# Moving the layer-norm writes from VectorE to ScalarE, and two additions to TensorE, in a transformer layer with a mixture of experts

## The chip, the cores and the metric

The kernel runs on one core of one Trainium2 chip. The metric is the device time in microseconds of the whole program; the median of three runs is compared. Nothing runs on the other cores.

## The reference, cut to what matters

The input holds 16 images of 4 x 128 x 256 numbers. `D` is 256, `P` is 128 tokens to an image, all in float32.

```python
h = tok(x)                                   # mix the 4 groups of an image with softmax weights
h = h + attn(layernorm(h), W_qkv, b_qkv, W_o, b_o)     # 16 causal heads of 16
n = layernorm(h)
scores = sigmoid(n @ gate_w.T) + gate_bias   # 64 experts, 4 of 8 groups, then the best 6
comb = top6 weights / (their sum + 1e-8)
h = h + shared(n) + sum_e comb_e * expert_e(n)
def layernorm(x): return (x - mean) / sqrt(var + 1e-5)
```

## The kernel before, in words

The program has two long stages. In the **image stage** a loop runs over steps `b = -2 ... 18`, written out in full. Step `b` holds a different part of the work for several images at once: `a` (b+3 on VectorE, b+2 on TensorE and ScalarE) is mixed, normed and projected to queries and keys, `v = b+1` gets its values, `b` goes through scores and softmax, `cc = b-1` through the output projection and the second norm, `d = b-2` through the gate and the choice of experts (`route`), and `e = b-3` gets its rows numbered (`place`) and scattered. Each engine has its own instruction stream with the steps in the same order, held together by semaphores. In the **tile stage** that follows, some 114 tiles of 128 scattered rows go through the experts, and a short end adds the six results of each token.

An engine works its stream strictly in the order written. What stands in one step, around the change:

- VectorE, step b: `nmax_of` (row maxima of the scores, two halves), `den_of`, `mix`, `place`, `normalise` (writes `o_sb` and sets `o_ready`), the rest of `mix`, `place` and `route`, the residual add into `h_all` after `proj_done`, the statistics (`bn_stats`, `bn_aggr` into `mv`), the last `route` parts, and at its end `apply` twice (L691): the normed input `xn` of image `a` (128x256), and `row`, the normed row of image `cc` written six times over, once for each chosen expert (128x1536, in one instruction; half of the four buffers lie in `xring`).
- GpSimd (POOL), step b: adds the output bias `bo_sb` to `h_all` (L401), makes `rs`, the inverse root of variance plus epsilon, from `mv` (`roots`, two instructions, L376 and L378), and issues six indirect DMAs that scatter the rows of image `e` (L393).
- TensorE, step b: scores, the turned attention output, the positions of the chosen rows (`pos_done`), the values, then the transposes of `row` for image `d` (L1184; they wait for `x2_ready` and, because they write the bank that `normalise` reads, for `o_ready`), of `xn`, and of `o_sb`; then gate, `turn_shift`, the output projection (`proj_done`), `keyed`, the projection to queries and keys, and the product with the values.
- ScalarE, step b: row sums of one or two images in steps up to 6 (`sum_image`, L440), the softmax of the token weights where a part of the images is due (`mixing_exp`, steps 1, 4 and 8), then copies out of PSUM (`vaug`, `x_sb`, `xnt`, `ont`), the gate's tanh, four exponentials (L475), four key copies (`kpair`, L481), `ot_sb`, and two query copies (`qt`, L488).

`place` makes a key per expert: position plus the expert's base `ebase`, then times the choice `sel_b`.

Of the kernel before, what the change touches and what calls it, by code (L numbers as in the profile page):

```python
# [13 lines left out]
P = 128  # L14
# [39 lines left out]
for _name, _n in (("ident", P), ("tri", P), ("tri_t", P), ("pick", GH), ("before", P), ("half", 2), ("ebase", E),  # L54
                  ("dest", NB * TOPK), ("spill", 1 + NY), ("upto", E), ("tile", NTAB)):
    C_AT[_name] = (_at, _n)
    _at += _n
# [9 lines left out]
def build(nc, x, w1t, b1, w2t, b2, wqkv, bqkv, wo, bo, gate, gbias, sgu, sd, wexp, const, out):  # L67
# [4 lines left out]
    with ExitStack() as ctx:  # L72
# [32 lines left out]
        bo_sb = sb("bo_sb", [P, D])  # L105
        gate_sb = sb("gate_sb", [P, KT, E])
# [17 lines left out]
        rs = sb("rs", [P, 2])  # L124
        rv = sb("rv", [P, 2])
        minus_half = sb("minus_half", [P, 2])
        xn = sb("xn", [P, 2, D])
# [23 lines left out]
        top8 = sb("top8", [P, 8])  # L151
# [5 lines left out]
        key0 = sb("key0", [P, E])  # L157
# [65 lines left out]
        for name in ("consts_ready", "sum_act", "sum_dve", "tok_chain", "tok_hid", "tok_tanh",  # L223
# [4 lines left out]
                     "o_transposed", "ont_ready", "bias_added", "proj_done", "ln_chain", "x2_ready", "var_ready", "root_ready", "var_eps", "half_set",  # L228
# [139 lines left out]
        def _(pool):  # L368
# [14 lines left out]
            for n in range(2):  # L383
                pool.wait_ge(S("var_ready"), n + 1)
                roots(n, n + 1, n + 1)
            pool.wait_ge(S("bias_joined"), 1)

            def step(b, par):
                v, e = b + 1, b - 3
# [41 lines left out]
        def _(act):  # L431
# [35 lines left out]
            def step(b, par):  # L467
# [112 lines left out]
        def _(dve):  # L580
# [20 lines left out]
            nc.vector.memset(shift_b[:], 0.0)  # L601
            nc.vector.memset(nt_f[:, 0:1], 1.0)
# [24 lines left out]
            def constants():  # L627
# [5 lines left out]
                nc.vector.tensor_copy(before_b[:], c("before"))  # L633
                nc.vector.tensor_copy(upto_b[:], c("upto", E)).then_inc(S("consts_ready"), 1)
# [90 lines left out]
            ROUTE = 12  # L725

            def route(d, q, k):
# [29 lines left out]
                elif k == 6:  # L757

                    done(nc.vector.max(top8[:], mk))
                elif k == 7:  # L760
                    done(nc.vector.match_replace(topr[:], top8[:], mk, -BIG))
                elif k == 8:
                    nc.vector.tensor_scalar(sel_b[:, q, :], topr[:, 0:E], -BIG, None, ALU.is_equal).then_inc(
                        S("sel_ready"), 1)
                    done(nc.vector.reduce_sum(tsum[:], top8[:, 2:8], axis=AX))
                elif k == 9:
                    done(nc.vector.tensor_scalar(tsum[:], tsum[:], 1e-8, None, ALU.add))
                elif k == 10:
                    done(nc.vector.reciprocal(tinv[:, q:q + 1], tsum[:]))
                elif k == 11:  # L770
# [658 lines left out]
```

## Time and profile before

| what | value |
|---|---|
| device time, median of 3 runs | 507.87 us (506.15 to 508.51) |
| profiled execution, its own time | 504.11 us |
| span of that execution, first to last instruction | 502.3 us |
| busy over the span | PE 86%, DVE 64%, ACT 43%, POOL 49% |
| mean granted TensorE clock | 0.954 of full speed |

The profiled execution is 1.8 us longer than its span, and 3.8 us under the median of the runs. The image stage fills about the first half of the span. Busy shares over the whole span mix the two stages, so a change in the image stage is read in that stage alone.

### The profile page before, as it was taken

How to read it: one execution, taken by the hardware profiler on the slowest of the kernel's cores; microseconds unless marked ns; L12 is line 12 of the kernel's file. 1: busy time of each engine (PE TensorE's matmuls, PEld its weight loads, DVE VectorE, ACT ScalarE, POOL GpSimd, SP SyncE). 2: the span in 40 equal slices, each digit the busy share in tenths (PEclk: the TensorE clock that was granted, in tenths of full speed). 3: DMA queues.
4: the chain of work that ended last, by engine and by line, in shares of the span. 5: the costliest groups of instructions: out<-in, count | busy, mean ns of one | idle time of the engine just before them, and what ended most of it. 6: DMA issues, size and time to landing. Idle time of an engine off the chain costs nothing.

```text
span 502.3 us, 13166 instructions
## 1 busy us (share of the span) xinstructions
PE 431.6 (86%) x3950; PEld 332.4 (66%) x3950; DVE 321.6 (64%) x1065; ACT 215.0 (43%) x662; POOL 246.4 (49%) x273
## 2 busy tenths in 40 slices
PE   1567889888988999778379999999999999976995
PEld 1446667666767776453258888888888888852653
DVE  3675789999899998877613444444444444430998
ACT  3254755564555556332014454454544544530000
POOL 1111115767666678767714656665565565560000
PEclk9988999998999999998769999999999999995999
DMA  8999971112111211222235687677577747643997
GB/s 273 336 351 296 302 210 54 66 65 77 65 64 59 73 66 65 87 85 85 105 105 164 197 244 256 185 213 240 177 237 232 232 138 221 215 132 106 409 407 271
DMA packets 56476, 90.00 MB, mean 179 GB/s; under 512 B 7719, under 2 KB 43690, under 8 KB 56400
## 3 DMA queue, kind: packets, MB, share of 16 engines
q1 hardware_dynamic: 44016, 61.69, 39.8%
q0 software_dynamic: 10080, 25.29, 14.2%
q10 hardware_dynamic: 2304, 2.10, 1.2%
q8 instruction: 37, 0.61, 0.5%
q14 instruction: 39, 0.32, 0.2%
HBM read 84.00 MB, written 40.82 MB: 248 GB/s over the span
## 4 chain that ended last, share of the span: by engine, by line
PE 27%; issue 8%; POOL 6%; DMA 5%; DVE 3%; SPq 1%; POOLq 0%; DVEq 0%
PE ps_low L1059 14%; PE ps L1059 8%; POOL y_rows L423 6%; PE ps_low L1305 3%; DMA x_sb<-y_rows 2%; DMA y_rows<-y,xring 2%; PE ps L1292 2%; DVE x_sb L816 1%; DVE x_sb L1037 1%; DVE x_sb L1054 1%; DMA slot_rows<-xring,slot_ix 1%; DVE h_all L1042 1%; DVE x_sb L1047 0%; DMA xring<-slot_rows 0%; POOL slot_rows L393 0%
## 5 line engine op out<-in xcount | busy, mean ns | idle before, releaser
L423 POOL DMA_INDIRECT y_rows<-y,xring x114 | 112.1, 984 | 89.7 <-issue 82.9
L1059 PE MATMUL ps_low<-wring,probt 128*128 x456 | 119.4, 385 | 0.0
L1020 DVE TENSOR_TENSOR probt<-probt,ps_low 128x128 f32<-128x128 f32 x114 | 32.7, 287 | 108.7 <-issue 89.5
L1059 PEld LDWEIGHTS ps_low<-wring,probt 128*128 128x128 f32 x456 | 78.8, 193 | 6.3 <-issue 0.2
L1059 PE MATMUL ps<-wring,probt 128*128 x228 | 68.2, 382 | 0.0
L560 ACT COPY probt<-ps_low 128x256 f32<-128x256 f32 x115 | 42.8, 372 | 49.3 <-PE ps_low L1305 48.3
L1013 DVE TENSOR_SCALAR y<-ps,xring 128x256 f32<-128x256 f32 x114 | 54.6, 479 | 6.4 <-DMA y_rows<-y,xring 5.1
L393 POOL DMA_INDIRECT slot_rows<-row,slot_ix x48 | 51.8, 1079 | 13.9 <-issue 13.4
L393 POOL DMA_INDIRECT slot_rows<-xring,slot_ix x48 | 51.6, 1076 | 14.0 <-issue 13.7
L565 ACT ACTIVATE probt<-ps_low 128x128 f32<-128x128 f32 x114 | 31.6, 277 | 58.0 <-PE ps_low L1059 58.0
L475 ACT ACTIVATE probt<-ps_low 128x512 f32<-128x512 f32 x64 | 33.1, 603 | 40.9 <-PE ps_low L1059 40.9
L1305 PE MATMUL ps_low<-const_sb,xring 128*128 128x128 f32 x230 | 44.9, 278 | 3.7 <-DMA xring<-slot_rows 3.6
L697 DVE TENSOR_REDUCE nmax<-ps_low 128x8 f32<-128x1024 f32 x32 | 38.9, 1215 | 7.2 <-PE ps_low L1059 7.1
L1305 PEld LDWEIGHTS ps_low<-const_sb,xring 128*128 128x128 f32 x230 | 32.5, 144 | 16.6 <-issue 4.7
L376 POOL TENSOR_SCALAR rv<-mv 128x2 f32<-128x2 f32 (+1 forms) x20 | 4.5, 223 | 79.3 <-DVE mv L844 66.5
L1059 PEld LDWEIGHTS ps<-wring,probt 128*128 128x128 f32 x228 | 34.4, 191 | 8.7 <-issue 0.3
L1059 PE MATMUL ps_low<-x_sb,sgu_sb 128*128 128x512 f32 x64 | 33.9, 682 | 6.5 <-issue 6.5
L1059 PE MATMUL ps<-xnt,wqkv_sb 128*128 128x128 f32 x256 | 35.4, 295 | 0.5 <-ACT xnt L508 0.5
L1059 PEld LDWEIGHTS ps<-xnt,wqkv_sb 128*128 128x128 f32 x256 | 32.2, 205 | 3.3 <-issue 2.6
L1292 PE MATMUL ps<-const_sb,probt 128*128 128x128 f32 x114 | 31.3, 275 | 0.2 <-DVE probt L1020 0.2
L554 ACT COPY probt<-ps 128x128 f32<-128x128 f32 x114 | 29.7, 260 | 0.7 <-PE ps L1292 0.6
L1059 PEld LDWEIGHTS ps_low<-x_sb,sgu_sb 128*128 128x128 f32 x64 | 13.9, 222 | 23.0 <-issue 22.7
(184 smaller groups left out, 731.5 us busy)
## 6 DMA issues: line engine op xcount, KB each, us to landing
wring<-wexp SPq DMA_DIRECT2D x115, 384.0 KB
xring<-slot_rows SPq DMA_DIRECT2D x115, 129.0 KB, 2.5
x_sb<-y_rows SPq DMA_DIRECT2D x16, 768.0 KB, 6.5
slot_rows<-pads SPq DMA_DIRECT2D x1, 8256.0 KB, 35.2
x_sb<-x SPq DMA_DIRECT2D x3, 2048.0 KB, 18.0
slot_rows<-pads SPq DMA_DIRECT2D x5, 516.0 KB, 9.9
x_sb<-x SPq DMA_DIRECT2D x4, 512.0 KB, 5.1
out<-h_all ACTq DMA_DIRECT2D x16, 128.0 KB, 5.4
```

Source lines behind the costliest of these rows:

```text
L393: nc.gpsimd.indirect_dma_start(out=slots_dram, out_offset=bass.IndirectOffsetOnAxis(ap=slot_ix[:, e % NROW, k:k + 1], axis=0), in_=row_of( ...
L423: nc.gpsimd.indirect_dma_start(out=y_dram, out_offset=bass.IndirectOffsetOnAxis(ap=xring[:, q, TO_AT:TO_AT + 1].bitcast(I32), axis=0), in_ ...
L475: nc.scalar.activation(probt[:, g].rearrange("p a k -> p (a k)"), psQ[g][:], ACT.Exp).then_inc(S("exp_done"), 1)
L554: nc.scalar.copy(ht[:, v % 2, :], ps[4 + v % 2][:, 0:P]).then_inc(S("ht_ready"), 1)
L560: nc.scalar.copy(xt[:, u % 2].rearrange("p a k -> p (a k)"), psT[u % 2][:, 0:D]).then_inc(S("xt_ready"), 1)
L565: nc.scalar.activation(silu[:, t % 2, :], psS[t % 2][:, 0:INTER], ACT.Silu).then_inc(S("silu_done"), 1)
L697: nc.vector.tensor_reduce(nmax[:, two, :], ps_low[:, two, :].rearrange("p g (a k) -> p g a k", a=GH), axis=AX, op=ALU.max, negate=True).th ...
L1013: nc.vector.tensor_scalar(y[:, a, :], ps[6 + v % 2][:, 0:D], xring[:, v % U, W_AT:W_AT + 1], None, ALU.mult).then_inc(S("y_ready"), 1)
L1020: nc.vector.tensor_tensor(hm[:, t % 2, :], silu[:, t % 2, :], psS[t % 2][:, INTER:2 * INTER], ALU.mult).then_inc(S("h_ready"), 1)
L1059: return nc.tensor.matmul(*a, **k)
L1292: nc.tensor.transpose(ps[4 + v % 2][:, 0:P], hm[:, v % 2, :], ident).then_inc(S("h_turned"), 1)
L1305: last = nc.tensor.transpose(psT[u % 2][:, k * P:(k + 1) * P], xring[:, uq, k * P:(k + 1) * P], ident)
```

## The change

- ScalarE instead of VectorE writes `xn` (from image 2 on) and the sixfold `row`, as Identity activations with per-partition scale `rs` and bias `mrs`, the product of the negative mean and `rs`. In ScalarE's stream they stand in step b after the sums and `mixing_exp` and ahead of the copy to `vaug`; `row` is that of image `d = b-2`, `xn` that of `a = b+2`.
- VectorE makes `rv` (variance plus epsilon) and `nm` (negative mean) itself; POOL makes `rs` and then `mrs`. Both are double buffered.
- The output bias comes from TensorE: one more matmul of ones with `bo_rows` (the bias in three bfloat16 terms on three partitions) at the start of the output projection. POOL no longer adds it, but splits it once, in ten instructions ahead of its loop.
- The base of the keys comes from TensorE too: one more matmul with `base_b` among those for the positions. `place` has one instruction less.
- The 1e-8 under the sum of the weights is a ninth column of the summed tile, so `route` has one instruction less. The order of some `place` and `mix` parts is changed.

```diff
-            def roots(lo, hi, n):
-                nc.gpsimd.tensor_scalar(rv[:, lo:hi], mv[:, lo:hi, 1], EPS, None, ALU.add).then_inc(S("var_eps"), 1)
-                pool.wait_ge(S("var_eps"), n)
-                nc.gpsimd.tensor_tensor(rs[:, lo:hi], rv[:, lo:hi], minus_half[:, lo:hi], ALU.pow).then_inc(
+            def roots(lo, hi, n, to):
+                nc.gpsimd.tensor_tensor(rs[:, to, lo:hi], rv[:, lo:hi], minus_half[:, lo:hi], ALU.pow).then_inc(
+                    S("rooted"), 1)
+                pool.wait_ge(S("rooted"), n)
+                nc.gpsimd.tensor_tensor(mrs[:, to, lo:hi], nm[:, lo:hi], rs[:, to, lo:hi], ALU.mult).then_inc(
                     S("root_ready"), 1)
...
+            split(nc.gpsimd.tensor_copy(bo_term[:, 0, :], bo_sb[:]), 1)
+            split(nc.gpsimd.tensor_tensor(bo_rest[:, 0, :], bo_sb[:], bo_term[:, 0, :], ALU.subtract), 2)
...
+            nc.gpsimd.tensor_tensor(bo_rows[:], bo_term[:, 0, :], bo_term[:, 2, :], ALU.add).then_inc(
+                S("bias_rows"), 1)
...
-                if has(v):
-
-                    pool.wait_ge(S("ln1_done"), v + 1)
-                    nc.gpsimd.tensor_tensor(h_all[:, v, :], h_all[:, v, :], bo_sb[:], ALU.add).then_inc(
-                        S("bias_added"), 1)
...
+                if has(a) and a >= 2:
+                    act.wait_ge(S("root_ready"), b + 3)
+                    wait(act, S("xn_transposed"), a - 1)
+                    nc.scalar.activation(xn[:, par, :], h_all[:, a, :], ACT.Identity, bias=mrs[:, q, 0:1],
+                                         scale=rs[:, q, 0:1]).then_inc(S("ln1_done"), 1)
+                if has(d):
+                    act.wait_ge(S("root_ready"), b + 3)
+                    wait(act, scattered[d % NROW], 16 * TOPK * (d // NROW))
+                    nc.scalar.activation(row_of(d)[:, :, 0:D], h_all[:, d, :].unsqueeze(1).to_broadcast([P, TOPK, D]),
+                                         ACT.Identity, bias=mrs[:, q, 1:2], scale=rs[:, q, 1:2]).then_inc(
+                        S("x2_ready"), 1)
...
+            def terms(lo, hi):
+
+                nc.vector.tensor_scalar(rv[:, lo:hi], mv[:, lo:hi, 1], EPS, None, ALU.add).then_inc(S("var_ready"), 1)
+                nc.vector.tensor_scalar(nm[:, lo:hi], mv[:, lo:hi, 0], -1.0, None, ALU.mult).then_inc(
+                    S("var_ready"), 1)
...
-                elif k == 9:
-                    done(nc.vector.tensor_scalar(tsum[:], tsum[:], 1e-8, None, ALU.add))
...
-                    nc.vector.tensor_tensor(key0[:], psC[:, 0:E], c("ebase"), ALU.add).then_inc(S("key_read"), 1)
+                    nc.vector.tensor_tensor(key[:], psC[:, 0:E], sel_b[:, q, :], ALU.mult).then_inc(S("key_read"), 1)
...
-                if has(a):
-                    dve.wait_ge(S("root_ready"), b + 4)
-                    wait(dve, S("xn_transposed"), a - 1)
-                    apply(image(h_all, a), xn[:, q, :], 0).then_inc(S("ln1_done"), 1)
-                if has(cc):
-                    dve.wait_ge(S("root_ready"), b + 4)
-                    wait(dve, scattered[cc % NROW], 16 * TOPK * (cc // NROW))
-                    apply(image(h_all, cc).unsqueeze(1).to_broadcast([P, TOPK, D]), row_of(cc)[:, :, 0:D], 1).then_inc(S("x2_ready"), 1)
...
+                    mm(psC[:, 0:E], ones_b[:], base_b[:], start=False, stop=False)
...
-                    both(psC[:, D:2 * D], lambda k: ont[:, k, :], lambda k: wo_sb[:, k, :]).then_inc(
-                        S("proj_done"), 1)
+                    if cc == 0:
+                        pe.wait_ge(S("bias_rows"), 1)
+                    mm(psC[:, D:2 * D], ones_b[:], bo_rows[:], start=True, stop=False)
+                    for k in range(KT):
+                        last = mm(psC[:, D:2 * D], ont[:, k, :], wo_sb[:, k, :], start=False, stop=k == KT - 1)
+                    last.then_inc(S("proj_done"), 1)
```

## Rows read from the trace of the kernel before

**Rows 1.** Windows: stretch, length, then busy us of PE, PEld, DVE, ACT, POOL; clock.

```profile
158.00:170.00 12.00, 10.83 (x175) 8.45 (x174) 11.78 (x42) 6.44 (x18) 8.66 (x10) 1.00 0.20 68
```

**Rows 2.** Timeline (start us, us, instruction, [idle before]) of VectorE, steps 9 to 10.

```profile
153.62 0.15 DVE L767 TENSOR_SCALAR tsum<-tsum 128x1 f32<-128x1 f32 x1
...
154.26 0.41 DVE L691 TENSOR_SCALAR xn<-h_all,mv,rs 128x256 f32<-128x256 f32 x1
154.59 1.07 DVE L691 TENSOR_SCALAR row<-h_all,mv,rs 128x1536 f32<-128x1536 f32 x1
155.57 1.22 DVE L697 TENSOR_REDUCE nmax<-ps_low 128x8 f32<-128x1024 f32 x1
...
157.29 0.41 DVE L721 TENSOR_TENSOR o_sb<-ps,rden 128x256 f32<-128x256 f32 x1
```

**Rows 3.** Timeline of TensorE, step 9 and the start of step 10.

```profile
146.13 0.41 PE L1184 MATMUL ps<-const_sb,xring 128*128 128x128 f32 x2 [1.72 <-DVE o_sb L721]
...
147.64 0.23 PE L1059 MATMUL ps<-ident_b,shift_b 128*128 128x128 bf16 x1
...
154.49 0.39 PE L1059 MATMUL ps_low<-tri_b,ident_b 32*32 32x512 bf16 x16
...
157.85 0.41 PE L1184 MATMUL ps<-const_sb,row 128*128 128x128 f32 x2 [1.38 <-DVE o_sb L721]
```

**Rows 4.** Timeline of ScalarE, step 9: first exponential, and the two queries.

```profile
150.64 2.07 ACT L475 ACTIVATE probt<-ps_low 128x512 f32<-128x512 f32 x4 [2.47 <-PE ps_low L1059]
...
154.40 0.70 ACT L488 ACTIVATE qt<-ps,bq_small 128x128 f32<-128x128 f32 x2
```

**Rows 5.** Timeline of POOL: first and last of the final 18 scatters.

```profile
228.19 0.96 POOL L393 DMA_INDIRECT slot_rows<-row,slot_ix  x1 [0.49 <-DVE row L808]
...
251.79 0.96 POOL L393 DMA_INDIRECT slot_rows<-xring,slot_ix  x1 [0.31 <-issue]
```

**Rows 6.** Lines view, ScalarE, 50 to 200 us: busy us, mean ns, idle.

```profile
L481 ACT ACTIVATE kpair<-ps,bk_half,const_sb 128x128 f32<-128x128 f32 x52 | 19.9, 492 | 0.0
...
L440 ACT ACTIVATE wring<-x_sb 128x1024 f32<-128x1024 f32 x6 | 6.6, 1106 | 0.1
...
L524 ACT CAST shift_t<-ps 128x128 bf16<-128x128 f32 x13 | 3.5, 267 | 0.5 <-PE ps L1059 0.5
```

**Rows 7.** Timeline of ScalarE, step 2: two sums, first copy, first exponential.

```profile
58.41 1.13 ACT L440 ACTIVATE wring<-x_sb 128x1024 f32<-128x1024 f32 x1
...
59.72 1.06 ACT L440 ACTIVATE wring<-x_sb 128x1024 f32<-128x1024 f32 x1
...
60.78 0.35 ACT L499 COPY vaug<-ps 128x256 f32<-128x256 f32 x1
...
65.35 1.09 ACT L475 ACTIVATE probt<-ps_low 128x512 f32<-128x512 f32 x2 [2.64 <-PE ps_low L1059]
```

**Rows 8.** Timelines, start of step 8: VectorE's maxima, ScalarE's token softmax.

```profile
130.74 1.20 DVE L697 TENSOR_REDUCE nmax<-ps_low 128x8 f32<-128x1024 f32 x1
...
133.07 0.22 ACT L452 ACTIVATE wexpd<-wshift 128x16 f32<-128x16 f32 x1 [2.51 <-DVE wshift L654]
```

**Rows 9.** Timeline of ScalarE: first exponential of steps 6, 7, 13 and 14.

```profile
112.47 2.06 ACT L475 ACTIVATE probt<-ps_low 128x512 f32<-128x512 f32 x4 [2.47 <-PE ps_low L1059]
...
126.10 1.08 ACT L475 ACTIVATE probt<-ps_low 128x512 f32<-128x512 f32 x2 [3.85 <-PE ps_low L1059]
...
196.59 2.06 ACT L475 ACTIVATE probt<-ps_low 128x512 f32<-128x512 f32 x4 [2.47 <-PE ps_low L1059]
...
207.56 2.07 ACT L475 ACTIVATE probt<-ps_low 128x512 f32<-128x512 f32 x4 [2.47 <-PE ps_low L1059]
```

**Rows 10.** Windows view, two stretches of step 7.

```profile
118.00:120.00 2.00, 0.57 (x3) 0.16 (x1) 1.90 (x11) 0.37 (x1) 1.60 (x2) 1.00 0.33 120
122.00:124.00 2.00, 2.00 (x8) 1.17 (x12) 2.00 (x8) 0.25 (x2) 1.70 (x2) 0.50 0.23 83
```

**Rows 11.** Timeline of POOL: the first bias addition.

```profile
25.52 0.77 POOL L401 TENSOR_TENSOR h_all<-h_all,bo_sb 128x256 f32<-128x256 f32 x1 [0.86 <-DVE bo_sb L960]
```

More of the change, by code:

```diff
@@ L53 @@
 C_AT = {}
-for _name, _n in (("ident", P), ("tri", P), ("tri_t", P), ("pick", GH), ("before", P), ("half", 2), ("ebase", E),
+for _name, _n in (("ident", P), ("tri", P), ("tri_t", P), ("pick", GH), ("before", P), ("half", 2), ("term", 3), ("ebase", E),
                   ("dest", NB * TOPK), ("spill", 1 + NY), ("upto", E), ("tile", NTAB)):
@@ L123, in build @@
         mv = sb("mv", [P, 2, 2])
-        rs = sb("rs", [P, 2])
+        rs = sb("rs", [P, 2, 2])
         rv = sb("rv", [P, 2])
+        nm = sb("nm", [P, 2])
         minus_half = sb("minus_half", [P, 2])
+        mrs = sb("mrs", [P, 2, 2])
         xn = sb("xn", [P, 2, D])
@@ L407, in step @@
                 if -2 < b <= NB:
-                    pool.wait_ge(S("var_ready"), b + 4 if b < 0 else 2 * b + 4 if b <= 12 else b + 16)
-                    roots(0 if has(b + 3) else 1, 2 if has(b - 1) else 1, b + 4)
+                    pool.wait_ge(S("var_ready"), 2 * b + 8)
+                    wait(pool, S("ln1_done"), min(b + 2, NB))
+                    wait(pool, S("x2_ready"), b - 2)
+                    roots(0 if has(b + 3) else 1, 2 if has(b - 1) else 1, b + 4, par)
                 if has(e):
@@ L841, in aggregate, with root_terms @@
                     at = ln[0]
+                    dve.wait_ge(S("root_ready"), b + 3)
                     for w in range(lo, hi):
                         dve.wait_ge(S("ln_chain"), at)
-                        nc.vector.bn_aggr(mv[:, w, :], st[:, w, :]).then_inc(S("var_ready"), 1)
+                        norm_step(nc.vector.bn_aggr(mv[:, w, :], st[:, w, :]))
+                def root_terms():
+                    dve.wait_ge(S("ln_chain"), ln[0])
+                    terms(lo, hi)
                 def placed(k):
@@ L910, in step @@
                 routed(6)
-                aggregate()
-                for k in range(7, ROUTE):
-                    routed(k)
-                if has(a):
-                    dve.wait_ge(S("root_ready"), b + 4)
-                    wait(dve, S("xn_transposed"), a - 1)
-                    apply(image(h_all, a), xn[:, q, :], 0).then_inc(S("ln1_done"), 1)
-                if has(cc):
-                    dve.wait_ge(S("root_ready"), b + 4)
-                    wait(dve, scattered[cc % NROW], 16 * TOPK * (cc // NROW))
-                    apply(image(h_all, cc).unsqueeze(1).to_broadcast([P, TOPK, D]), row_of(cc)[:, :, 0:D], 1).then_inc(S("x2_ready"), 1)
+                if hi > lo:
+                    aggregate()
+                routed(7)
+                if hi > lo:
+                    root_terms()
+                for k in range(8, ROUTE):
+                    routed(k)
                 if b in PART_AT:
@@ L935, in first_norm @@
                 dve.wait_ge(S("ln_chain"), n + 1)
-                nc.vector.bn_aggr(mv[:, n, :], st[:, n, :]).then_inc(S("var_ready"), 1)
+                nc.vector.bn_aggr(mv[:, n, :], st[:, n, :]).then_inc(S("first_stats"), 1)
+                dve.wait_ge(S("first_stats"), n + 1)
+                terms(n, n + 1)
             def first_apply(n):
@@ L1394 @@
     put("half", p[:, None] // HD % 2 == np.arange(2)[None, :])
-    put("ebase", np.arange(E)[None, :] * REGION + P + 1)
+    put("term", p[:, None] == np.arange(3)[None, :])
+    base = np.arange(E) * (REGION // P)
+    put("ebase", np.concatenate([np.stack([base // 16 * 16 * P, base % 16 * P, np.full(E, P + 1)]),
+                                 np.zeros((P - 3, E), np.int64)], 0))
     at = (np.arange(NB)[None, :, None] * P + p[:, None, None]) * TOPK + np.arange(TOPK)
```

70 lines of the change are left out of this document (40 added, 30 removed).

## The prediction

> **What bounds the kernel now.** I read the windows first: in a stretch of 12.00 us of the image stage VectorE is busy for 11.78, TensorE for 10.83, ScalarE for 6.44 and POOL for 8.66 [rows 1]. VectorE is full, ScalarE half empty. Then the timelines of one step, engine by engine, because a full engine can be replaced as the bound by a loop through several engines.
>
> I use two marks in a step. X is when TensorE starts to transpose the normed rows (146.13 in step 9, 157.85 in step 10: a period of 11.72 us) [rows 3]. E is when ScalarE starts the first exponential, 150.64 in step 9, so X to E takes 4.51 us, all TensorE work in order [rows 3, 4]. TensorE had waited 1.38 us for VectorE's `o_sb` before X [rows 3]; it is not the bound, but it is not far from it. ScalarE goes from E through exponentials, keys, `ot_sb` and queries; the pair of queries starts at 154.40 and takes 0.70, and if the second starts 0.27 us after the first, ScalarE can start the next thing at 154.94, 4.30 us after E [rows 4]. In the old kernel it then has time to spare.
>
> At the end of the stage POOL issues its last 18 scatters without a gap worth naming (228.19 to 251.79; one wait of 0.49) [rows 5]. The tile stage begins when they have landed, and nothing in it changes: a delay of the image stage goes to the end whole.
>
> **What the change takes from VectorE.** The two `apply` fill 154.26 to 155.57, 1.31 us; the epsilon is a small instruction of 0.15, and the key base another, taken as 0.15 too; `rv` and `nm` come back, two of 0.15 [rows 2]. Net -1.3 us: VectorE's own loop goes from 11.7 to some 10.4 us. If that were all, a dozen steps would give 15 us. It is not all, since two loops through other engines stand right behind.
>
> **Loop through TensorE and VectorE.** From X the scores end at 154.49 + 0.39 = 154.88, 8.75 us later [rows 3]. The bias matmul adds something between 0 and the 0.23 us that a bfloat16 matmul of 128 columns lasts [rows 3]; I take 0.15. (The matmul for the key base falls in TensorE's wait and costs nothing.) VectorE's maxima start some 0.07 later; from their start at 155.57 to the next X at 157.85 there are 2.28 us [rows 2, 3], through `o_sb`. Sum: 8.75 + 0.15 + 0.07 + 2.28 = 11.25 us. Step 13 checks it, where VectorE has no mixing left: E to E is 207.56 - 196.59 = 10.97 [rows 9]. So an idle VectorE gives at most half a microsecond a step.
>
> **Loop through TensorE and ScalarE.** The new activations stand in ScalarE's stream behind the queries of the step before and ahead of X. The trace has no such row, so bounds: key copies with scale and bias by partition take 492 ns for 128 columns, a plain copy of 128 columns 267, so the two pointers cost some 0.22; a sum over 1024 columns takes 1106, so a column costs (1106 - 267)/896 = 0.94 ns [rows 6]. `row`, 1536 columns, is then 1106 x 1.5 = 1.66 to 0.492 + 1408 x 0.00094 = 1.81 us; I take 1.7, nearest to the sum's row, and keep 1.6 to 1.9. `xn` is 0.3 to 0.6; I take 0.5. Together 2.2 (1.9 to 2.5). With 0.07 for the semaphore: E + 4.30 + 2.2 + 0.07 to X, then 4.51 + 0.15 to E: 11.23 us.
>
> By the Trainium skill, ScalarE: Activation LUTs (What ACT_TABLE_LOAD costs), an activation takes 186 ns plus 0.833 per column plus 93 per pointer operand, 1.65 us for `row`: an estimate of the same loop at 11.2. Its Rules for kernel authors name VectorE for plain multiply and add; the trace agrees for this tile, VectorE writes the row in 1.07 us [rows 2]. No number here hangs on these two sentences.
>
> So steps without other work on ScalarE go at about 11.25 instead of about 11.7. But not all steps are such.
>
> **The sums are no longer hidden.** In steps 2 to 6 ScalarE first sums images: two take from 58.41 to 60.78, one 1.31 us by the spacing [rows 7]. Before, they lay in ScalarE's spare time ahead of X; now `row` stands behind them, so that cover is gone and each lies on the loop.
> - Step 2: sums end at 60.78, so X is 60.78 + 2.2 + 0.07 = 63.05 and E 67.71, against 65.35 [rows 7]: +2.4.
> - Steps 3, 5, 6: 11.23 + 1.31 = 12.54 each, 37.6.
> - Steps 4 and 8: `mixing_exp` also stands ahead of `row`, and it waits for VectorE in that same step. In step 8 the maxima start at 130.74, 4.64 after E of step 7, and the exponential at 133.07 [rows 8, 9]; with 0.12 for it, X is 2.45 + 2.27 = 4.72 after the maxima. E to E: 4.64 + 4.72 + 4.66 = 14.0 each, 28.0.
> - Step 7: 11.25 plus four small chained instructions of the last token part ahead of `o_sb`, at 0.18 each as an estimate from the 0.15 of such a one [rows 2] and a semaphore: 12.0.
> - Steps 9 to 13: 11.25 each, 56.2.
>
> Sum from E of step 2 to E of step 13: 133.8, against 196.59 - 65.35 = 131.24 [rows 7, 9]: +2.5. With step 2's +2.4 and 0.15 of bias matmul in steps 14 and 15: +5.2.
>
> **The clock.** Step 7 took 126.10 - 112.47 = 13.63 us [rows 9], where 11.72 + 0.72 would do: 1.2 too much. In 118 to 120 TensorE was busy for 0.57 of 2.00 us, and in 122 to 124 its granted clock was 0.50, 1.2 GHz instead of 2.4 [rows 10]. The waits ahead of X become longer: in sum steps 1.38 grows to about 2.1, in step 2 to 3.1. I count one such drop, as the old kernel has: +1.2. Total +6.4.
>
> **At no cost.** POOL's ten split instructions at 0.77 [rows 11] keep it some 8.5 us, from 25.5 to 34; the scale for image 2 waits for that, but its reader on ScalarE stands behind the sum of image 8 (1.31 [rows 7]); without that cover it costs at most 0.9. POOL's product for `mrs` takes the place of its `rv`. VectorE's statistics end before 153.6 [rows 2]; with two terms and POOL's two instructions, some 1.1, the scale is there by 154.7, just ahead of ScalarE (154.94); if later, every step takes that much longer. In steps 14 and 15 there is no `xn`, no key copy and no query, so ScalarE reaches `row` early. In the last steps `row` comes 0.6 later, under POOL's queue of scatters [rows 5]; if POOL were not behind, +0.6. The wait for `x2_ready` that VectorE gets at its step's end is for a row written early in that step. Queued behind ScalarE's wait for `root_ready` are `vaug` and the copies after X; TensorE waits for these, which is the loop above.
>
> **The rivals.**
> - *The clock falls more often.* Six steps (2, 3, 4, 5, 6, 8) get waits of 2 to 3 us before X. If each is followed by a drop at 1.2 us, not one but six: 5.2 + 7.2 = +12.4, 520.3. For it: the drop in step 7 followed a wait of 1.6 [rows 10]. Against: the wait of 1.38 in step 10 had none; the clock stayed at 1.00 [rows 1, 3]. The Trainium skill, TensorE: Matmul & The Clock Gate (Part 1), says that the slow clock is the default and recent activity releases it; the rows of step 7 agree.
> - *Short activations, and no drop.* With 1.9 for both, six steps save 0.3 each and step 7 has no drop: 5.2 - 1.8 = +3.4, 511.3; if the bias matmul costs nothing as well (13 x 0.15, but only where ScalarE's loop binds, some 1.0), +2.4, 510.3, the edge of no change.
> - *The other side: faster.* ScalarE reaches the row in time everywhere. X by VectorE's path comes at E + 4.24 + 0.07 + 2.28 = E + 6.59, so from the queries' end there are 2.2 us. If sums, exponential and both writes fit in them, all eleven steps go at 11.25 plus 2.1 for the token parts: 125.9, -5.3, with the bias +0.3: 502.9. For it: without sums the writes just fit. Against: a sum alone takes 1.31 and the stream is in order [rows 7].
> - *It doesn't do what it says:* the loops come out as long as VectorE's was, about 508. That takes a cancellation of gain and loss.
>
> **How the numbers follow.** The sum is made against the profiled 504.11, which is 3.8 under the median of the runs; the difference is put on the median: 507.87 + 6.4 = 514.3. Chances: this case, one or two drops, 511.5 to 517.5: 0.5; more drops: 0.2; short activations: 0.14; faster: 0.1; nothing: 0.06. The longer bound (2.5 for both writes) gives 13 x 0.3 = 3.9 more, 518.2. The range 509 to 521 leaves out the faster case and some of the unchanged one. A change of 0.5% (2.5 us) is about what a measurement can tell from none: faster 0.1; same, from the last case and part of the short one, 0.14; slower 0.76.
>
> **What would show it.** VectorE's busy share in the image stage falls to near 0.85 and it waits for the scores at its step's start. ScalarE has `row` at about 1.7 us, and TensorE's wait before X is put down to it in steps 2 to 8, with steps of 12.5 and, twice, 14. Steps 9 to 13 go at 11.2 to 11.3. Wrong would be: X still waiting for `o_sb` in steps 3 to 6; `row` much shorter or longer than 1.7; the stage won or lost ahead of step 2 or behind step 13.

## The result: 3.1% slower, more than predicted

The changed kernel takes 523.04 us in the median of five runs (516.92 to 523.97), the kernel before 507.87 (504.96 to 509.64 in five): a ratio of 1.0307, interval 1.0265 to 1.0348. The prediction was 514.3, range 509 to 521. The direction was right; the time lies outside the range. Medians and ratios leave out the few executions of any of these kernels that came out far longer than the rest (735.31 us once for the kernel before).

The profiled execution is the fastest of the five: 516.92 us, span 514.5, against 504.11 and 502.3, so +12.8. Its granted clock averages 0.944; the other four lie between 0.922 and 0.933. No profile shows where those lose 5 to 7 us more. What follows explains the 12.8.

The page of the changed kernel: VectorE, at 64% before, is at 57%, and TensorE's clock row has seven slices at 8 among its first 16 where it had three.

```profile
span 514.5 us, 13270 instructions
PE 439.2 (85%) x3982; PEld 338.7 (66%) x3982; DVE 291.1 (57%) x1045; ACT 246.8 (48%) x692; POOL 234.4 (46%) x267
...
PEclk9988989888989999998668999999999999997899
```

**Where the time went, step by step.** Intervals from the first exponential of the step before to that of the step named (E to E, us), read from ScalarE's timeline as in [rows 9]. "Filled", "late", "order" and "best" are the runs e3, e2, e9 and e11 below.

| step | before | predicted, without clock | after | filled | late | order | best |
|---|---|---|---|---|---|---|---|
| 2 | 11.21 | 13.57 | 14.56 | 13.28 | 11.20 | 14.50 | 11.01 |
| 3 | 11.89 | 12.54 | 12.14 | 13.72 | 12.13 | 12.04 | 11.63 |
| 4 | 11.85 | 14.0 | 15.05 | 13.73 | 12.19 | 15.02 | 11.86 |
| 5 | 11.66 | 12.54 | 13.46 | 12.04 | 11.51 | 13.45 | 11.09 |
| 6 | 11.72 | 12.54 | 13.44 | 12.04 | 11.44 | 12.04 | 11.00 |
| 7 | 13.63 | 12.0 | 12.25 | 13.85 | 12.27 | 11.74 | 11.81 |
| 8 | 12.48 | 14.0 | 15.07 | 13.68 | 12.18 | 16.16 | 11.85 |
| 9 | 12.06 | 11.25 | 11.51 | 11.54 | 11.50 | 11.02 | 11.01 |
| 10 | 11.72 | 11.25 | 11.43 | 11.43 | 11.44 | 11.00 | 11.00 |
| 11 | 11.49 | 11.25 | 11.44 | 11.44 | 11.44 | 11.31 | 11.30 |
| 12 | 11.49 | 11.25 | 11.43 | 11.43 | 11.43 | 11.18 | 11.17 |
| 13 | 11.25 | 11.25 | 11.01 | 11.00 | 11.00 | 11.00 | 11.01 |

E of step 13 lies at 207.88, before at 196.59: +11.3. POOL's last scatter is issued at 263.30, before at 251.79 [rows 5]: +11.5. The rest of the span adds 0.7 and the time around it 0.6. So the loss is in the image stage, most of it in the steps with sums or token softmax ahead of the row.

```profile
263.30 0.96 POOL L415 DMA_INDIRECT slot_rows<-xring,slot_ix  x1 [0.30 <-issue]
```

ScalarE's timeline of steps 2 and 3, answering to [rows 7]. In step 2 two sums stand ahead of `xn` and `row`, in step 3 one (73.93 to 74.97: 1.04 by the spacing, from the start of one instruction to that of the next). `row` takes 1.65 and 1.74.

```profile
59.37 1.13 ACT L459 ACTIVATE wring<-x_sb 128x1024 f32<-128x1024 f32 x1
...
61.74 0.58 ACT L517 ACTIVATE xn<-h_all,mrs,rs 128x256 f32<-128x256 f32 x1
62.23 1.65 ACT L522 ACTIVATE row<-h_all,mrs,rs 128x1536 f32<-128x1536 f32 x1
...
69.65 2.07 ACT L494 ACTIVATE probt<-ps_low 128x512 f32<-128x512 f32 x4 [3.02 <-PE ps_low L1094]
...
73.93 1.13 ACT L459 ACTIVATE wring<-x_sb 128x1024 f32<-128x1024 f32 x1
...
74.97 0.67 ACT L517 ACTIVATE xn<-h_all,mrs,rs 128x256 f32<-128x256 f32 x1
75.46 1.74 ACT L522 ACTIVATE row<-h_all,mrs,rs 128x1536 f32<-128x1536 f32 x1
...
81.79 0.60 ACT L494 ACTIVATE probt<-ps_low 128x512 f32<-128x512 f32 x1 [2.50 <-PE ps_low L1094]
```

TensorE's timeline at X of steps 2, 3, 4, 5 and 8, answering to [rows 3]: it waits for ScalarE's row, not for `o_sb`.

```profile
63.94 0.69 PE L1219 MATMUL ps<-const_sb,row 128*128 128x128 f32 x2 [3.15 <-ACT row L522]
77.25 0.44 PE L1219 MATMUL ps<-const_sb,row 128*128 128x128 f32 x2 [1.47 <-ACT row L522]
91.08 0.61 PE L1219 MATMUL ps<-const_sb,xring 128*128 128x128 f32 x2 [2.32 <-ACT xring L522]
104.43 0.44 PE L1219 MATMUL ps<-const_sb,xring 128*128 128x128 f32 x2 [1.73 <-ACT xring L522]
...
145.22 0.44 PE L1219 MATMUL ps<-const_sb,xring 128*128 128x128 f32 x2 [2.26 <-ACT xring L522]
```

Windows behind these waits, answering to [rows 10]; the clock is the number after POOL's busy time.

```profile
64.00:67.00 3.00, 3.00 (x14) 2.87 (x15) 0.45 (x3) 1.64 (x6) 0.00 (x0) 0.50 1.11 285
76.00:79.00 3.00, 1.75 (x13) 1.40 (x14) 2.93 (x11) 2.59 (x6) 0.00 (x0) 1.00 0.01 3
91.00:94.00 3.00, 2.92 (x14) 2.73 (x15) 1.23 (x4) 1.77 (x7) 1.57 (x2) 0.54 0.29 102
106.00:109.00 3.00, 3.00 (x29) 2.26 (x32) 2.33 (x11) 0.60 (x3) 0.62 (x1) 0.62 0.19 62
118.00:121.00 3.00, 3.00 (x15) 2.59 (x16) 2.38 (x11) 1.56 (x6) 1.71 (x2) 0.59 0.28 100
145.00:148.00 3.00, 2.78 (x14) 2.48 (x15) 1.48 (x6) 1.89 (x7) 1.54 (x2) 0.64 0.31 106
```

Five steps (2, 4, 5, 6, 8) have a drop, a fall of the granted clock from 1.00 to 0.50 (2.4 to 1.2 GHz), behind the wait. Step 3, with the wait of 1.47, has none (the second line). In the kernel before, steps 2 to 13 had one drop, in step 7.

Steps 9 to 12 have no sums, and here VectorE's relief ought to show. The window that answers to [rows 1] (the third busy time is VectorE's), then the timelines of VectorE and of TensorE, answering to [rows 2, 3]:

```profile
158.00:170.00 12.00, 10.97 (x177) 8.46 (x175) 9.76 (x40) 8.50 (x21) 6.45 (x8) 1.00 0.16 57
```

```profile
166.96 1.23 DVE L735 TENSOR_REDUCE nmax<-ps_low 128x8 f32<-128x1024 f32 x1 [2.17 <-PE ps_low L1094]
...
168.67 0.42 DVE L759 TENSOR_TENSOR o_sb<-ps,rden 128x256 f32<-128x256 f32 x1
169.01 1.22 DVE L735 TENSOR_REDUCE nmax<-ps_low 128x8 f32<-128x1024 f32 x1
...
170.27 0.40 DVE L743 CAST shift_b<-nmax 128x16 bf16<-128x16 f32 x1
170.34 0.48 DVE L719 SCALAR_TENSOR_TENSOR h_all<-x_sb,wtok,h_all 128x256 f32<-128x256 f32 x1
170.74 0.17 DVE L745 TENSOR_TENSOR shift_b<-nmax,shift_b 128x16 bf16<-128x16 f32 x1
```

```profile
166.41 0.39 PE L1094 MATMUL ps_low<-tri_b,ident_b 32*32 32x512 bf16 x16
...
169.24 0.41 PE L1219 MATMUL ps<-const_sb,row 128*128 128x128 f32 x2 [0.81 <-DVE o_sb L759]
...
170.97 0.23 PE L1094 MATMUL ps<-ident_b,shift_b 128*128 128x128 bf16 x1 [0.20 <-DVE shift_b L745]
171.06 0.27 PE L1094 MATMUL ps<-bo_rows,ones_b 128*128 128x256 bf16 x1
171.17 1.03 PE L1094 MATMUL ps<-wo_sb,ont 128*128 128x256 f32 x4
...
177.85 0.40 PE L1094 MATMUL ps_low<-tri_b,ident_b 32*32 32x512 bf16 x16
```

VectorE, busy for 11.78 of 12 us before, is busy for 9.76 and waits 2.17 us for the scores: it is no bound any more. But the step lasts 11.43, not 11.25, and `turn_shift` (TensorE's transpose of `shift_b`) waits for `shift_b`. The chain: scores end at 166.80, first maxima 166.96, second maxima 169.01, cast, a mixing piece of 0.40 by the spacing, second part of `shift_b` at 170.74, `turn_shift` at 170.97; from there 7.28 us of TensorE work to the next scores' end at 178.25 (177.85 and 0.40). That is 11.45, the step's length to 0.02. The prediction had followed the chain through `o_sb` and never priced this one. And the change itself puts that mixing piece, `mixed(1)`, between the two parts of the shift; before, it stood behind them.

ScalarE's lines, 50 to 200 us, answering to [rows 6]: the two forms of `row`, and `xn`, whose spacing to `row` is 0.49.

```profile
L522 ACT ACTIVATE row<-h_all,mrs,rs 128x1536 f32<-128x1536 f32 x6 | 10.3, 1722 | 0.0
L522 ACT ACTIVATE xring<-h_all,mrs,rs 128x1536 f32<-128x1536 f32 x5 | 8.5, 1702 | 0.0
...
L517 ACT ACTIVATE xn<-h_all,mrs,rs 128x256 f32<-128x256 f32 x11 | 7.1, 648 | 0.0
```

The start loses 0.95 (E of step 1 at 55.09 against 54.14). POOL's timeline, then ScalarE's: the split, answering to [rows 11], ends at 33.58, and the root for image 2 and its product `mrs`, done at 34.38, stand behind it. But ScalarE's `xn` for that image starts at 34.91 without idle time, right behind the sum ahead of it. So the split did not hold it up, and where the 0.95 comes from is not shown.

```profile
25.96 0.45 POOL L398 CAST bo_term<-bo_sb 128x256 bf16<-128x256 f32 x1 [0.84 <-DVE bo_sb L995]
...
32.91 0.67 POOL L407 TENSOR_TENSOR bo_rows<-bo_term 128x256 bf16<-128x256 bf16 x1
33.54 0.57 POOL L381 TENSOR_TENSOR rs<-rv,minus_half 128x1 f32<-128x1 f32 x1
34.19 0.19 POOL L384 TENSOR_TENSOR mrs<-nm,rs 128x1 f32<-128x1 f32 x1
```

```profile
34.91 0.62 ACT L517 ACTIVATE xn<-h_all,mrs,rs 128x256 f32<-128x256 f32 x1
```

### The profile page after: what moved, and what is told of

Read it like the earlier page. It is cut to its first block and busy times, and to the rows that moved or that the text cites. A ratio compares the mean times of both kernels' runs of the same rounds, so it can differ in the third digit from the quotient of the medians.

```text
span 514.5 us, 13270 instructions
## 1 busy us (share of the span) xinstructions
PE 439.2 (85%) x3982; PEld 338.7 (66%) x3982; DVE 291.1 (57%) x1045; ACT 246.8 (48%) x692; POOL 234.4 (46%) x267
## 5 line engine op out<-in xcount | busy, mean ns | idle before, releaser
L381 POOL TENSOR_TENSOR rs<-rv,minus_half 128x2 f32<-128x2 f32 (+1 forms) x20 | 13.1, 654 | 95.7 <-DVE nm L729 95.7
L415 POOL DMA_INDIRECT slot_rows<-row,slot_ix x48 | 48.6, 1012 | 17.0 <-issue 16.5
L415 POOL DMA_INDIRECT slot_rows<-xring,slot_ix x48 | 48.2, 1005 | 17.1 <-issue 15.6
L500 ACT ACTIVATE kpair<-ps,bk_half,const_sb 128x128 f32<-128x128 f32 x64 | 24.5, 489 | 5.9 <-PE ps L1094 5.9
```

The lines of the kernel that those rows point to most:

```text
L415: nc.gpsimd.indirect_dma_start(out=slots_dram, out_offset=bass.IndirectOffsetOnAxis(ap=slot_ix[:, e % NROW, k:k + 1], axis=0), in_=row_of( ...
```

## The experiments

Claim 1: work ahead of `row` in ScalarE's stream delays X. Claim 2: the long waits of TensorE before X bring clock drops on top. Claim 3: behind both, the loop through `shift_b` keeps the steps at 11.43, whoever writes the rows. The letters of theories in the recorded expectations belong to each text alone. Ratios are to the kernel before on the same chip.

### e1: the sums behind the shift's copy

```diff
-                for img in ACT_SUMS.get(b, ()):
-                    sum_image(img)
+                if b < 2:
+                    for img in ACT_SUMS.get(b, ()):
+                        sum_image(img)
...
                     nc.scalar.copy(shift_t[:], psO[:, 0:P]).then_inc(S("shift_copied"), 1)
+                    if b > 1:
+                        for img in ACT_SUMS.get(b, ()):
+                            sum_image(img)
```

> The changed kernel with one thing moved: the image sums of steps 2 to 6 stand behind the copy to shift_t in ScalarE's stream, where the changed kernel has 2.5 us without work ahead of the exponentials, and no longer ahead of xn and row. Same work on every engine. Theory A (the loop of TensorE and ScalarE, with what stands ahead of row on it, and clock drops that follow the longer waits): steps 3, 5 and 6 go from 12.1 to 13.5 to about 11.4, step 2 loses 2.3, the drops in steps 2, 5 and 6 go away; step 4 keeps its wait for the token softmax; 8 to 10 us faster than the changed kernel, so about 511 to 514 beside 507.9 for the kernel before. Theory B (the added instructions themselves, the matmuls or POOL's product, make each step longer): the same time as the changed kernel, 520 or more. Theory C (the clock falls by chance or by load, not by the waits): 6 us faster from the sums, with as many drops as before.

Measured: 514.90 us, ratio 1.0163 (1.0107 to 1.0218), just above the 511 to 514 that were expected. Steps 2, 3, 5 and 6 go from 14.56, 12.14, 13.46, 13.44 to 11.20, 12.14, 11.51, 11.44. Steps 4 and 8, where `mixing_exp` is still ahead, stay at 15.07 and 14.83, each with its drop. Step 7 has a drop behind a wait of 1.39 for `o_sb`. Claim 1 holds, except for step 3: it does not shrink, since there another loop, with X waiting 0.98 for `o_sb`, is just as long.

### e2: `mixing_exp` behind the row as well

```diff
-                if b > 1 and b - 1 in PART_AT:
-                    mixing_exp(PART_AT[b - 1])
...
                         S("x2_ready"), 1)
+                if b > 1 and b - 1 in PART_AT:
+                    mixing_exp(PART_AT[b - 1])
```

> As the run with the sums moved, and the token softmax of steps 4 and 8 also stands behind row. Theory A: steps 4 and 8 go from 15.1 to about 11.5 to 12.2, and their clock drops go; every step from 2 on at 11.4 to 12.2; about equal to the kernel before, 506 to 510. Theory B: no gain by the position.

Measured: 505.14 us, ratio 0.9982 (0.9947 to 1.0017): the whole loss is gone. Steps 4 and 8 are 12.19 and 12.18, and no drop is left in steps 2 to 13. ScalarE still writes every row. So the writes on ScalarE cost nothing by themselves; the blocks that stood ahead of them in the stream did. And the result is only level with the kernel before, though VectorE is relieved: that speaks for claim 3.

### e3: TensorE kept busy during the waits

Extra matmuls, whose result nobody reads, ahead of the wait for the row; nothing else of the change is touched.

```diff
+        FILL = {2: 36, 3: 16, 4: 26, 5: 20, 6: 20, 8: 26}
...
+                    for _ in range(FILL.get(b, 0)):
+                        mm(psO[:, P:2 * P], ones_b[:], before_b[:], start=True, stop=True)
                     pe.wait_ge(S("x2_ready"), d + 1)
```

> The changed kernel with 16 to 36 extra bfloat16 matmuls of 128 columns in steps 2 to 6 and 8, on TensorE ahead of its wait for row, into a part of PSUM that nothing reads; they fill the wait and leave X where it is. Theory A with the clock behind the waits: the granted clock stays at 1.00 in steps 2 to 8 apart from one step at most, each step loses 1.0 to 1.4 us, 4 to 7 us faster than the changed kernel (about 516). Theory C (the clock falls by load): the same drops or more, the same time. If the extra matmuls are too many, X is later and the time is longer at a clock of 1.00.

Measured: 510.49 us, ratio 1.0095 (1.0059 to 1.0131). Windows of the same steps 2, 4 and 5 as above:

```profile
64.00:67.00 3.00, 2.23 (x15) 1.85 (x16) 0.82 (x4) 2.31 (x7) 0.00 (x0) 1.00 1.11 318
...
91.00:94.00 3.00, 2.13 (x20) 1.62 (x18) 1.95 (x8) 2.57 (x7) 2.39 (x3) 1.00 0.27 92
106.00:109.00 3.00, 3.00 (x73) 2.33 (x72) 2.94 (x15) 0.52 (x3) 0.99 (x1) 1.00 0.27 94
```

The clock stays at 2.4 GHz, and steps 2, 4, 5, 6 and 8 lose 1.28, 1.32, 1.42, 1.40 and 1.39: 6.8 us for the five drops. ScalarE's order is unchanged, and X comes as long after the E before it as in the changed kernel (8.84, 9.29, 7.59, 7.59 and 9.23 us); what shrinks is X to E, from 5.7 to 5.9 us to 4.44 to 4.45. Claim 2 holds for these five steps. The Trainium skill, TensorE: Matmul & The Clock Gate (Part 1), says that the slow clock is the default and that activity releases it; this run agrees, since activity without use bought the time. Steps 3 and 7 got longer (13.72, 13.85). In step 3 TensorE stood still inside a group of matmuls, waiting for nothing that the profile names:

```profile
73.58 1.14 PE L1096 MATMUL ps_low<-kpair,qt 32*128 32x256 f32 x13 [0.90 <-issue]
```

Step 7 has a drop of its own. The profiled execution is the longest of its ten runs (515.92), so only its image stage is read here: E of step 13 lies 2.8 us earlier than in the changed kernel. The ratio fell by 2.1%, some 11 us; the profile does not show where the others gained more.

### e4: TensorE's and POOL's part alone

The kernel before with bias and key base by TensorE, no bias on POOL, the ninth column, and the changed order of VectorE; VectorE still writes `xn` and `row`. The split stands behind a root, at step -1.

```diff
+                    mm(psC[:, 0:E], ones_b[:], base_b[:], start=False, stop=False)
...
+                    mm(psC[:, D:2 * D], ones_b[:], bo_rows[:], start=True, stop=False)
...
-                    nc.gpsimd.tensor_tensor(h_all[:, v, :], h_all[:, v, :], bo_sb[:], ALU.add).then_inc(
-                        S("bias_added"), 1)
```

> The kernel before with the TensorE part alone: output bias and key base by TensorE, no bias addition on POOL, the epsilon as a ninth column; VectorE still writes xn and the six rows, POOL still makes the root. The splitting of the bias stands behind the root of step -1. Theory A: VectorE loses 0.3 to 0.4 a step and is still the bound, the loop of TensorE and VectorE is at 11.25; 2 to 5 us faster than the kernel before, 503 to 506. Theory B (the added matmuls make each step longer): slower than the kernel before by 2 us or more.

Measured: 505.32 us, ratio 0.9982 (0.9948 to 1.0016), within the expected 503 to 506 but no gain that can be told from none. Steps 9 to 12 are 11.51, 11.43, 11.44, 11.43, the same as in the changed kernel and in e2, with 1.3 us more work on VectorE (busy for 11.04 of the 12 us from 158 to 170, against 9.76); `turn_shift` waits 0.20 for `shift_b`. The floor does not depend on who writes the rows: claim 3. With the extra matmuls the kernel is no slower than before.

### e5 and e6: an unused sum in steps 9 to 12, before and after

```diff
+                if 9 <= b <= 12:
+                    act.wait_ge(S("sum_act"), summed[0])
+                    summed[0] += 1
+                    nc.scalar.activation(junk, x_sb[:, NB - 1, :, :].rearrange("p g d -> p (g d)"), ACT.Identity,
+                                         accum_out=dummy_sum[:, b - 9:b - 8]).then_inc(S("sum_act"), 1)
```

In the kernel before:

> The kernel before with one more image sum of 128x1024, whose result nobody reads, at the start of ScalarE's steps 9 to 12. Theory A: these sums lie in ScalarE's spare time ahead of X; steps 9 to 12 keep 11.5 to 12.1, first exponential of step 9 to that of step 13 stays at 46 us. Theory B or any view by busy shares: no change either, so this is the control for the next run.

In the changed kernel:

> The changed kernel with the same extra sum at the start of ScalarE's steps 9 to 12. Theory A: each of these steps gets 1.0 to 1.3 us longer, 11.43 to about 12.5, plus about 1.1 wherever the clock drops after the longer wait: first exponential of step 9 to that of step 13 from 45.3 to 49.5 to 54. A view by busy shares (ScalarE is free for half of each step): no change.

Measured, one run each: before with the sums 505.8 us, E of step 9 to E of step 13 45.98 against 45.95; hidden. After with the sums 526.57; steps 9 to 12 take 13.61, 13.63, 13.64, 13.64 against 11.51, 11.43, 11.44, 11.43: +2.2 each, for a sum of 1.04 by the spacing. X comes 0.92 later after the E before it (7.59 against 6.67 in steps 10 to 12), and the rest, 1.26 to 1.3 from X to E, goes with the drop that each of these steps now has. TensorE's wait, and the window behind it, of the changed kernel with the sums:

```profile
185.35 0.44 PE L1225 MATMUL ps<-const_sb,row 128*128 128x128 f32 x2 [1.73 <-ACT row L528]
```

```profile
187.00:190.00 3.00, 3.00 (x25) 2.17 (x28) 2.86 (x14) 0.33 (x2) 0.00 (x0) 0.50 0.12 44
```

The same instruction is free on one side of the change and costs twice its length on the other. The wait's length alone does not decide on the drop: [rows 3] have a wait of 1.72 in step 9 of the kernel before, without one. Up to step 8 the kernel of e6 is the changed kernel, and its step 6 has the same wait (1.73, X at 117.92 against 117.89), but no drop, and takes 12.04 instead of 13.44. The window is that of 118 to 121 above, where the clock was 0.59:

```profile
118.00:121.00 3.00, 3.00 (x32) 2.28 (x36) 2.83 (x13) 1.48 (x6) 1.74 (x2) 1.00 0.28 100
```

Step 6 of e9 is the same (1.72, no drop, 12.04). So the price of a drop, 1.40, shows without any filler too, and claim 2 holds for most long waits, not for each. In both runs the low clock of step 8 lasts twice as long (15.92 and 16.16 instead of 15.07). In e5 the one drop of the kernel before falls in step 5 instead of 7, behind a wait of 1.31 for `o_sb`.

### e7: one row ahead of X, five copies after

```diff
-                    nc.scalar.activation(row_of(d)[:, :, 0:D], h_all[:, d, :].unsqueeze(1).to_broadcast([P, TOPK, D]),
+                    nc.scalar.activation(row_of(d)[:, 0, 0:D], h_all[:, d, :],
...
+                    nc.scalar.copy(row_of(d)[:, 1:TOPK, 0:D],
+                                   row_of(d)[:, 0:1, 0:D].to_broadcast([P, TOPK - 1, D])).then_inc(S("six_ready"), 1)
```

> The changed kernel, but ScalarE first writes one of the six copies of the normed row (128x256), the one that TensorE transposes, and the other five later, between the copy to shift_t and the exponentials. The sums and the token softmax stay ahead. Theory A: ScalarE's loop loses about 1.1 us; steps 9 to 13 are then bound by the loop of TensorE and VectorE, 11.2 to 11.3; steps 3, 5 and 6 at about 11.4, without drops; steps 4 and 8 keep a longer wait, about 12.9; 8 to 11 us faster than the changed kernel, 510 to 514. Theory B: no gain, the work is the same.

Measured: 511.24 us, ratio 1.0101 (1.0036 to 1.0166). Steps 4, 5, 6 and 8 come down to 12.61, 11.56, 11.43 and 12.60, without a drop; step 2 keeps one (13.81), and step 3 gets one (13.74), behind a wait of 1.25 for `o_sb`, where about 11.4 was expected. A shorter row lets four of the five steps escape; steps 9 to 12 stay at 11.43 to 11.55, as claim 3 has it.

### e8: all three moves, split of the bias at step -1

The edits of e1, e2 and e7 together, and POOL's split, taken from ahead of the loop, behind its root of step -1.

```diff
                     roots(0 if has(b + 3) else 1, 2 if has(b - 1) else 1, b + 4, par)
...
+                if b == -1:
+                    split_bias()
```

> The changed kernel with all that the theory asks for: sums and token softmax behind row, one row first and five copies later, and the split of the bias behind the root of step -1. Theory A: every step at 11.2 to 11.4 (7 and 8 about 12), start 0.6 to 0.9 us earlier, one clock drop or none in steps 2 to 13; 3 to 6 us faster than the kernel before, 502 to 505. If the gain stays out, the loop of TensorE and VectorE is longer than 11.25.

Measured: 507.51 us, ratio 1.0021 (0.9989 to 1.0053), not the expected 502 to 505. From step 4 to step 12 the steps are 11.43 to 12.3 without a drop, but E of step 1 comes at 59.37, 4.3 later than in the changed kernel. Why is not shown: POOL is idle for 2.63 us between the end of the split (39.31) and its next root, so no root waited for the split.

```profile
41.94 0.57 POOL L381 TENSOR_TENSOR rs<-rv,minus_half 128x1 f32<-128x1 f32 x1 [2.63 <-DVE nm L744]
```

### e9: VectorE's order alone

```diff
-                mixed(0)
                 placed(0)
...
-                placed(1)
                 if has(b):
                     shift_of(b, 0)
-                mixed(1)
+                placed(1)
                 if has(b):
                     shift_of(b, 1)
+                mixed(0)
                 placed(2)
+                mixed(1)
```

> The changed kernel with VectorE's order alone altered: the two mixing pieces mixed(0) and mixed(1) go behind the second part of the shift, and placed(1) goes between its two parts. Nothing else is touched. In the changed kernel steps 9 to 12 take 11.43 us each and turn_shift waits for VectorE's shift_b. Theory: the loop there closes through shift_b; with 0.4 us of mixing taken out of that path, steps 9 to 12 fall to 11.0 to 11.2 us, where ScalarE's loop or o_sb is next, and turn_shift no longer waits for shift_b. Steps 2 to 8, which wait for ScalarE's row, keep their 12 to 15 us. Rival: the floor of 11.43 is set by o_sb and the longer chain of matmuls; then steps 9 to 12 stay within 0.05 us of 11.43.

Measured, one run: 516.13 us. Steps 9 to 12: 11.02, 11.00, 11.31, 11.18 instead of 11.43; `turn_shift` waits for nothing, and X waits for ScalarE's row. Claim 3 is shown: an edit of VectorE's order, no work less, takes 0.3 us from a step in the mean. What is next is the loop through ScalarE's row, which the prediction had put at 11.23 and which takes 11.0 to 11.3.

```profile
178.19 0.41 PE L1219 MATMUL ps<-const_sb,row 128*128 128x128 f32 x2 [0.76 <-ACT row L522]
```

### e10 and e11: everything together, with split and with whole rows

The edits of e1, e2 and e9, and POOL's split behind its root of step 0; e10 has also that of e7, e11 writes the six rows in one instruction as the change does.

```diff
-                if b == -1:
+                if b == 0:
                     split_bias()
```

> All that the runs suggest together: the changed kernel with the image sums of steps 2 to 6 and mixing_exp behind the copy of the shift, one of the six normed rows written ahead of X and the other five copied from it between the shift's copy and the exponentials, VectorE's order with the shift ahead of the mixing, and POOL's split of the bias moved behind its root of step 0. Theory: ScalarE's stream ahead of X shrinks by some 1.2 us and the loop through shift_b by 0.4, so steady steps take 10.9 to 11.1 us instead of 11.43, no clock drop in steps 3 to 12, first exponential of step 2 near 65.3, and the whole 498 to 502 us, faster than the kernel before by 1.0 to 1.8%. Rival: the floor of 11.43 stays (o_sb binds next), and it comes out at 503 to 507 us, no change.

> The same as the run before it with the six rows in one instruction ahead of X, as the change has them. If the loop through ScalarE (queries, xn, row at 1.7 us, X, scores, exponential) is next behind the one through shift_b, steady steps take 11.15 to 11.25 us and the whole is 1 to 2.5 us slower than with the split row; if o_sb is next, the two are equal.

Measured: e10 500.74 us, ratio 0.9897 (0.9868 to 0.9927); e11 499.02, ratio 0.9875 (0.9833 to 0.9917), 1.2% faster than the kernel before. The intervals overlap, so the two can't be told apart. In e11 steps 9 to 12 take 11.0 to 11.3 and X waits for the row; in e10 10.93 to 11.01, and X waits 0.58 for `o_sb`. TensorE's X, first of e11, then of e10:

```profile
173.06 0.44 PE L1226 MATMUL ps<-const_sb,xring 128*128 128x128 f32 x2 [0.86 <-ACT xring L524]
```

```profile
174.60 0.41 PE L1234 MATMUL ps<-const_sb,xring 128*128 128x128 f32 x2 [0.58 <-DVE o_sb L774]
```

In the two profiles the split row is 1.0 us shorter from E of step 0 to E of step 13 (149.55 against 150.54), as expected, but its whole is not: its first E is at 40.54 against 38.15, and behind E of step 13 it loses another 2.0, most of it in step 15, which has a drop (12.21 against 10.65). So the expectation that e11 would be the slower one is not borne out; why the start differs is open.

### e12: the order without ScalarE's writes

The kernel of e4 with the order of e9 and the split behind the root of step 0: VectorE writes all rows. Against e4:

```diff
-                if b == -1:
+                if b == 0:
                     split_bias()
...
-                mixed(0)
                 placed(0)
...
-                placed(1)
                 if has(b):
                     shift_of(b, 0)
-                mixed(1)
+                placed(1)
                 if has(b):
                     shift_of(b, 1)
+                mixed(0)
                 placed(2)
+                mixed(1)
```

> The kernel before with the bias and key base by TensorE (as in the run of that part alone, the split now behind POOL's root of step 0) and VectorE's order of the run with the order altered; VectorE still writes the normed inputs and all six rows, ScalarE nothing new. In the run of that part alone VectorE waited 0.27 us for POOL's root and 0.58 for the scores in steps of 11.43, so its own work is some 10.6 us. Theory: with the loop through shift_b shortened by 0.4 us, steady steps take 11.0 to 11.1 us, where o_sb is next, and the whole is 497 to 501 us: moving the writes to ScalarE was not needed for the gain. Rival: VectorE's own work with the wait for the root is next, and steps stay at 11.3 to 11.45, 503 to 506 us; then the writes on ScalarE are worth some 0.4 us a step once the order is right.

Measured: 502.05 us, ratio 0.9933 (0.9899 to 0.9967), between the theory's 497 to 501 and the rival's 503 to 506. Step 9 has a drop (13.43); 10 to 13 take 10.93, 11.30, 11.03, 10.83. X waits for `o_sb`, and VectorE, which does not wait for the scores in these steps, 0.28 for the root:

```profile
177.86 0.41 PE L1196 MATMUL ps<-const_sb,xring 128*128 128x128 f32 x2 [0.64 <-DVE o_sb L740]
```

```profile
174.51 0.41 DVE L710 TENSOR_SCALAR xn<-h_all,mv,rs 128x256 f32<-128x256 f32 x1 [0.28 <-POOL rs L381]
```

So about half of e11's gain, by the two ratios, needs no write on ScalarE at all. Whether the other half (0.9933 to 0.9875, on two chips, with intervals that overlap) is the writes or the drop in step 9 is not settled.

## Why the prediction was wrong

**The step that failed** is "I count one such drop, as the old kernel has: +1.2." There were five. They cost 6.8 us (e3, step by step) where 1.2 was put in. It was the rival "the clock falls more often", +12.4; the profiled execution shows +12.8. The argument against it, a wait of 1.38 without a drop, was about a shorter wait than the sum steps get. But five drops alone give 507.87 + 5.2 + 6.8 = 519.9, still inside the range. Of the other 3.1 us of the median the profiled execution has 0.8 (12.8 against 12.0); the rest is in executions that were not profiled, and its cause stays open. That the profile had five was in part chance: step 6 escaped its drop in e6 and e9.

**The rest, without the clock,** was +5.2 predicted. Measured with e3's steps 2, 4, 5, 6 and 8 and the changed kernel's others: E of step 13 is 11.3 - 6.8 = 4.5 us later than in the kernel before, whose own drop in step 7 is in that number. Up to that point the prediction has 2.4 + 2.5 = 4.9. So the sum was nearly right, partly by luck, since 0.95 of the 4.5 is the start and several terms were off:

- *Sums on the path:* right in mechanism (e1). Steps 5 and 6 are 12.04 without a drop, not 12.54: one sum costs 1.04, not 1.31, and X to E takes 4.45, not 4.66. In step 3 the sum was hidden (e1: 12.14 with and without).
- *Steps 4 and 8:* 13.7 without a drop (e3), 14.0 predicted; that `mixing_exp` was on the path is shown by e2.
- *`row` and `xn`:* 1.72 and 1.70, and 0.49 by the spacing; 1.7 and 0.5 predicted. The estimate by the Trainium skill, ScalarE: Activation LUTs (What ACT_TABLE_LOAD costs), 1.65, lies within 0.07 of it.
- *Steps 9 to 12:* 11.43, not 11.25. The predicted loop through `o_sb` was there with a wait of 0.81, but the one through `shift_b` closed later. +0.2 a step.
- *The semaphores*, 0.07 each, had no row behind them: from the row's end to X there are 0.05 (75.46 + 1.74 to 77.25), from the scores' end to the maxima 0.16 (166.80 to 166.96).
- *The start* was taken as nothing, and 0.95 is lost there. It is not POOL's split, as the prediction feared with "at most 0.9": `xn` did not wait for it.
- *The bias matmul* takes 0.11 by the spacing (171.06 to 171.17), 0.15 predicted.
- *At no cost:* the key base by TensorE (e4); the tail, where the last scatter is late by what E of step 13 is late, and 0.2.

**The rival on the other side** (faster, 502.9) had the right idea of what the writes would do in ScalarE's spare time. What was missing for it was the place in the stream: with sums and `mixing_exp` behind the row (e2) the same writes cost nothing. Even then the gain was nil until the order on VectorE was mended (e9, e11).

**What stays open:** why the four runs that were not profiled took 5 to 7 us more at a lower mean clock (more drops would fit, none was seen); what besides a wait's length decides on a drop; what lengthens the start, where the first E differs by up to 4 us among the variants.

## What to carry to other kernels

Work that is free in an engine's stream stops being free when something on the critical loop is queued behind it: before moving an instruction into a half-empty engine, list what stands ahead of it in every kind of step, and put the movable blocks behind it. On TensorE price such a delay with the clock: here each sum of 1.04 us cost 2.2 (e6). And before relieving a full engine, follow every chain that passes through it, each tile by itself: here the chain through `shift_b`, with the mixing piece that the change put into it, gave steps 0.06 to 0.3 us shorter than the full engine had (steps 10 to 12), and a change of order gave what the relief could not.

## What the runs showed of the hardware

- Matmuls without a use, 20 in step 5, made the kernel faster: they held the granted clock at 1.00 and the step got 1.4 us shorter (e3).
- The same instructions with the same wait of TensorE, 1.73 us in step 6, were followed by a drop in the changed kernel (13.44 us) and by none in e6 (12.04).
- In e8, with POOL's split under way, two instructions that overlap were both longer than elsewhere: POOL's addition took 0.87 us (0.67 in the changed kernel, at 32.91 above) and VectorE's on 128x16 elements 0.63 (0.17 in the changed kernel, at 170.74 above). The kernel before has one of these at 0.68 too (step 8, 134.84), of which only the last 0.13 us lie beside a POOL addition, so whether the overlap is the cause is open. POOL's timeline, then VectorE's:

```profile
38.44 0.87 POOL L408 TENSOR_TENSOR bo_rows<-bo_term 128x256 bf16<-128x256 bf16 x1
```

```profile
38.70 0.63 DVE L760 TENSOR_TENSOR shift_b<-nmax,shift_b 128x16 bf16<-128x16 f32 x1
```
